# A two-layer decoder on one core: products of the identity with itself where the plan of work gives TensorE nothing

## What is computed

```python
x = _layernorm(x + _L0_attn_ref(x, ...))            # attention by random features
x = _layernorm(x + _L0_xattn_ref(x, ctx_768, ...))  # attention over the text, then an MLP
x = _layernorm(x + _L0_ffn_ref(x, ...))             # router, 8 experts with capacity, top 2
x = _layernorm(x + _L1_attn_ref(x, ...))            # causal attention by a Taylor expansion
x = _layernorm(x + _L1_xattn_ref(x, ctx_768, ...))  # attention over the text, 16 heads of 64
x = _layernorm(x + _L1_ffn_ref(x, ...))             # causal attention, then 4 dense experts
```

## Time and profile before

| | us |
|---|---|
| median of 3 runs | 1166.63 |
| the 3 runs | 1166.63, 1165.93, 1173.93 |
| span of the profiled execution | 1165.0 |
| PE busy | 1001.8 (86%) |
| DVE busy | 640.4 (55%) |
| ACT busy | 588.3 (50%) |
| POOL busy | 284.6 (24%) |
| share of the chain that ended last: PE, DVE, ACT | 56%, 19%, 11% |

### The profile page before, as it was taken

One profiled execution on the slowest core, in us unless ns is written; L12 is line 12 of the kernel. 1 busy time (PEld: TensorE's weight loads), 2 busy tenths in 40 slices (PEclk: granted clock), 3 DMA queues, 4 the chain that ended last, 5 costly groups with the idle time before them and its releaser, 6 DMA issues.

```text
span 1165.0 us, 21556 instructions
## 1 busy us (share of the span) xinstructions
PE 1001.8 (86%) x8624; PEld 707.4 (61%) x8624; DVE 640.4 (55%) x1519; ACT 588.3 (50%) x1374; POOL 284.6 (24%) x292
## 2 busy tenths in 40 slices
PE   7996898887689988789998799889888897789995
PEld 4664565665388854456655676667666665447654
DVE  3246545666669833454455476776676664527003
ACT  5532565552468844344544354556555544465741
POOL 2521412100500033211112202221132124132733
PEclk9988889898989999899999988999999888679998
DMA  9341464102679785422252243313222105000001
GB/s 311 99 86 40 112 127 110 45 12 98 209 272 314 259 278 168 139 88 85 80 173 88 81 120 105 101 34 107 81 57 78 27 1 226 1 1 1 1 1 32
DMA packets 66676, 123.68 MB, mean 106 GB/s; under 512 B 11632, under 2 KB 41968, under 8 KB 62496
## 3 DMA queue, kind: packets, MB, share of 16 engines
q1 hardware_dynamic: 64528, 117.48, 33.0%
q0 software_dynamic: 2048, 4.82, 1.4%
HBM read 86.30 MB, written 35.92 MB: 105 GB/s over the span
## 4 chain that ended last, share of the span: by engine, by line
PE 56%; DVE 19%; ACT 11%; DMA 5%; issue 4%; POOL 4%; SPq 1%; another core or an unknown queue 0%; DVEq 0%; ACTq 0%; POOLq 0%
PE psum L398 38%; DVE s_p L2695 3%; ACT s_p L2653 3%; POOL rs L2985 2%; PE psum L2612 2%; DVE s_max L2684 2%; PE psum L2623 2%; PE psum L1369 2%; PE psum L2784 1%; DVE s_pT L2676 1%; PE psum L550 1%; DVE s_max L653 1%; PE psum L2173 1%; PE psum L2159 1%; PE psum L2604 1%
## 5 line engine op out<-in xcount | busy, mean ns | idle before, releaser
L2653 ACT ACTIVATE s_p<-psum,s_max 112x375 f32<-112x375 f32 x128 | 72.3, 569 | 87.6 <-DVE s_max L2684 87.6
L693 POOL TENSOR_TENSOR rstd<-meanvar,minus_half 112x1 f32<-112x1 f32 x40 | 23.1, 578 | 279.6 <-DVE meanvar L645 209.9
L653 DVE TENSOR_REDUCE s_max<-psum 112x2 f32<-112x750 f32 x64 | 59.4, 935 | 32.5 <-PE psum L550 31.4
L2985 POOL TENSOR_TENSOR rs<-ms,minus_half 112x32 f32<-112x32 f32 x8 | 43.5, 5442 | 110.3 <-DVE ms L2919 110.3
L398 PE MATMUL psum<-Wv,ctx 128*125 128x512 f16 x240 | 59.6, 392 | 11.2 <-ACT s_v L624 5.4
L398 PE MATMUL psum<-ctx,Wk 128*128 128x375 f16 x320 | 62.8, 331 | 5.0 <-ACT s_yT L2242 2.8
L2684 DVE TENSOR_REDUCE s_max<-psum 112x1 f32<-112x375 f32 x128 | 63.7, 539 | 2.3 <-PE psum L2604 2.1
L2612 PE MATMUL psum<-ident,s_p 112*125 112x112 f32 x384 | 61.4, 294 | 3.9 <-DVE s_p L2695 2.3
L609 ACT ACTIVATE s_k<-psum 128x375 f16<-128x375 f32 x64 | 31.2, 488 | 62.1 <-PE psum L398 59.5
L2604 PE MATMUL psum<-s_k,s_q 64*112 64x375 f16 x384 | 46.0, 345 | 17.0 <-ACT s_p L2653 6.5
L2612 PEld LDWEIGHTS psum<-ident,s_p 112*125 112x125 f32 x384 | 51.7, 198 | 13.7 <-DVE s_p L2695 3.9
(11 more groups left out here) (360 smaller groups left out, 2445.1 us busy)
## 6 DMA issues: line engine op xcount, KB each, us to landing
keys<-s_k SPq DMA_DIRECT2D x64, 187.5 KB, 2.2
s_k<-keys SPq DMA_DIRECT2D x8, 1500.0 KB, 7.6
values<-s_v SPq DMA_DIRECT2D x48, 224.0 KB
s_v<-values SPq DMA_DIRECT2D x16, 672.0 KB
raw_wg<-in_wg SPq DMA_DIRECT2D x8, 1024.0 KB, 6.6
raw_wu<-in_wu SPq DMA_DIRECT2D x8, 1024.0 KB, 7.1
raw_wd<-in_wd SPq DMA_DIRECT2D x8, 1024.0 KB
s_kd<-k_halves SPq DMA_DIRECT2D x48, 93.8 KB, 3.8
```

Source lines behind the costliest of these rows:

```text
L653: VE.tensor_reduce(s1_max[b % 2][:, 2 * p:2 * p + 2], rings["s1"][unit][0:N, :, 0:S], X, ALU.max, negate=True).then_inc(*V.up("max1", n))
L2653: SC.activation(rings["p4"][2 * n + j], rings["s4"][(n, j)][0:N, 0:S], ACT.Exp, bias=s4_max[b % 2][:, h:h + 1], accum_out=s4_sum[b % 2][:, ...
L2985: GP.tensor_tensor(rs5[b % 2][:], ms5[b % 2][:], minus_half[:], ALU.pow).then_inc(*G.up("rs5", b))
```

## The change

`weave` gets a parameter `idle` with the name of a ring. Whenever all strands have passed once, and some bank of that ring is free by the plan, it places a unit `("warm", i)` that takes a bank of that ring. In TensorE's program such a unit waits for the last reader of the bank and issues five products of the identity (128x128, f32) with 64 of its own columns into the bank. Nothing reads them; the unit has no mark, and the bank counts as free again at once. The three `weave` calls of stages 1, 3 and 4 pass `misc1`, `misc3` and `misc4`. Nothing else moves: apart from the inserted products PE's order is the same, and so is that of DVE, ACT, POOL and SyncE. The plan places 61 such units, 305 matmuls of the program: 19 in stage 1, 12 in stage 3, 30 in stage 4.

```diff
+    WARM = 5
+    warm_units = (("warm", i) for i in itertools.count())
+    step("warm", bank="warm")
+
-    def weave(*streams, filler=iter(())):
+    def weave(*streams, filler=iter(()), idle=None):
...
                 hurry[0] = passed >= len(live)
+                if idle and passed == len(live) and any(
+                        all(name in r.value for r, name in freed) for freed in rings[idle].freed):
+                    rings["warm"] = rings[idle]
+                    place(next(warm_units))
                 units = next(stream, "end")
...
+    def keep_busy(unit, ring):
+
+        pe.wait_ge(*ring.free(unit))
+        for _ in range(WARM):
+            TE.matmul(ring[unit][:, 0:64], ident[:], ident[:, 0:64], start=True, stop=True)
...
-          follow(s1_queries, range(2, B, 2)))
+          follow(s1_queries, range(2, B, 2)), idle="misc1")
...
-            if what == "v1":
+            if what == "warm":
+                keep_busy(unit, rings["misc1"])
+            elif what == "v1":
...
-          filler=keys4)
+          filler=keys4, idle="misc3")
...
-          s5_split())
+          s5_split(), idle="misc4")
```

More of the change, by code:

```diff
@@ L2136, in tensor_s3 @@
             what, *at = unit
-            if what == "qk3":
+            if what == "warm":
+                keep_busy(unit, rings["misc3"])
+            elif what == "qk3":
                 b, c = at
@@ L2594, in tensor_s4 @@
             what, *at = unit
-            if what == "sc4":
+            if what == "warm":
+                keep_busy(unit, rings["misc4"])
+            elif what == "sc4":
                 n, = at
```

## The result

Slower: 1211.9 us, median of four runs (1194.8 to 1225.0), against 1166.7 for the kernel before, run beside it (four runs, 1165.9 to 1173.9). The ratio is 1.0263, 95% interval 1.0184 to 1.0342: clear of no change, but it does not decide whether the loss is over 2%. Times 1166.7 the ratio is 1197 us. The profiled execution of the changed kernel took 1214.1 us with a span of 1212.2.

What follows compares the result with a forecast made beforehand. PE, busy 86% of the span with 56% of the last chain, was taken as the bound; 1165.0 + 10.5 + 6.6 + 2.0 = 1184.1 us profiled, with 1.6 for the median of runs 1185.7, range 1169 to 1206.

Steps and rivals of the forecast that it cites:

- The price of a unit: Everywhere: ten traced products with their weight loads take 1.1 us at 2.4 GHz, 2.1 at 1.2 GHz.
- The reading of the eight router products: End of stage 1: eight router products take 0.95 us; weight loads, 0.11 us each, set the pace, not the columns.
- the first rival: All three ends: products stream at the columns' pace, a unit costs 0.6 us, 1164 us in all; chance 0.15.
- End of stage 1, +10.5: 11 units before the last router product add 8.9 us, four units ahead of them 1.6; sum +10.5 us.
- The rival that stage 2 absorbs the delay: Stage 2 waits for expert weights or values rather than the router, so 1175 us; chance 0.07.
- End of stage 3, +6.6: Five units before the `w_Wo` products add 4.0 us, three later ones 2.6; the clock is high, nothing to win back.
- End of stage 4, +2.: Units add 2.6 us at `w_wo` and 2.2 behind it; stage 6 gives back 2.0 and 0.8; sum +2.0 us.
- if the units hold the clock at 2.4 GHz: End of stage 4, ahead of `w_wo`: with the clock held, busy time at 1.2 GHz shrinks, winning 12.0 us.
- the rival that they do not: End of stage 4: thin products don't hold the clock, 1220 us, or 1203 for half of it; chance 0.15 together.
- The reading of the clock: From the profile rows: the clock falls after waits of 1 to 3 us and is high where products are dense.
- Behind it, -2.0 and -0.8: Stage 6: first 12 products drop from 4.44 to about 2.2 us (-2.0); the 36 from 1031.79 give -0.8.
- The bank waits: Stages 1 and 3: units make PE wait for unneeded bank readers, tenths each, 1190 us; counted within the forecast's 0.60.

Runs made afterwards that it cites:

- narrow kernel: Changed kernel with 64 stationary identity columns instead of 128, units at all three ends: 1166.8 us in one run; timed again, median 1179.9, ratio 0.9982 to before.
- narrow units in stage 4 alone: Units of five f32 products with 64 stationary columns instead of 128, only at the end of stage 4: ratio 0.9954 to before, median 1167.5 us.

## Why the forecast was right, and where it was too low

Direction and most of the mechanism came out as forecast: units fill the waits, what does not fit into them delays the path, and each end stands for itself. What did not is that the units would hold the clock at the end of stage 4. The forecast was 1185.7 us, +19.1 on the profiled execution. By ratio the changed kernel took 1197, inside the range of 1169 to 1206; the plain median of its four runs, 1211.9, lies above it. The working, step by step:

- **The price of a unit**, 1.1 us at 2.4 GHz and 2.1 at 1.2: measured 1.10 and 2.05 to 2.09. The reading of the eight router products held, and with it the first rival fell: no unit of the changed kernel is near 0.6. The narrow kernel shows why. The isolated gap of the Trainium skill, "TensorE: Matmul & The Clock Gate", section "Back-to-back issue gap", would have made a unit as cheap as that bound or cheaper; the same section says that this gap counts too little for small products, since it leaves out the weight loads, and the 0.11 us per product measured here agrees with that.
- **End of stage 1, +10.5:** +9.7. The last router product ends 9 us later than the start of the stretch alone would put it, the `out` product that ran at the low clock took 1.93 where it had 3.48, the value products behind the five last units took 3.40 where they had 5.72, and those five units cost next to nothing, as forecast. The granted clock over this end is 1.00, where before some 10 of its 36.7 us ran at 1.2 GHz; even with that gain it is longer. The rival that stage 2 absorbs the delay fell with the run that has units in stage 1 alone.
- **End of stage 3, +6.6:** +7.4. There was no low clock to win back, as forecast.
- **End of stage 4, +2.** This is the term that was mis-sized: +11.8 up to the first product of stage 6 where the steps had +4.8 (2.6 and 2.2), and +1 to +4 behind it where they had -2.8. The parts can be read from the stretches. The units: forecast 30 x 1.1 = 33; in the trace 26 at 1.10 and four at 2.07, 37.0. The idle time filled: forecast 14.8 + 2.2 less 0.8 of latency, 16.2; measured 18.8 - 4.0 = 14.8. The clock: forecast 12.0 back; PE's work other than units went from 37.1 to 63.7 - 37.0 = 26.7, so 10.4 came back. 37.0 - 14.8 - 10.4 = 11.8. The difference of 7.0 is 4.0 + 1.4 + 1.6, and the first and the last of these have one cause: 17.1 us of the stretch ran at 1.2 GHz in one piece, four units among them. The step that failed is "if the units hold the clock at 2.4 GHz"; I named the rival that they do not, and gave it 0.15, but let no part of its price into the sum. The step was true by half: 37 us low before, 18 after.
- **The reading of the clock.** The prediction says that the clock falls after waits of 1 to 3 us. The rows are not that simple: at the end of stage 3 waits up to 2.45 us left it at 1.00, while in the changed kernel it fell at 1032.4, and the only wait of the 10 us ahead of it is one of 0.68 us. The second pair of rows is the same place in the kernel with narrow units in stage 4 alone, where PE idled longer and the clock stayed up:

```profile
1031.52 1.04 PE L2804 MATMUL psum<-k,q 32*112 32x224 f32 x8 [0.68 <-ACT e_up L2851]
1032.49 0.99 PE L2807 MATMUL psum<-mask,ident 112*112 112x448 bf16 x2
```

```profile
999.66 1.01 PE L2804 MATMUL psum<-k,q 32*112 32x224 f32 x8 [1.21 <-ACT e_up L2851]
1000.60 0.58 PE L2807 MATMUL psum<-mask,ident 112*112 112x448 bf16 x2
```

- **Behind it, -2.0 and -0.8:** the first twelve products took 4.64 us, still at 1.2 GHz, in a low stretch of 17 us of their own; nothing came back. No kernel of the table has stage 6 below 136.8 us, so at most 0.3 of these 2.8 us came back anywhere. In the kernel with units in stage 4 alone the low stretches there are shorter (10 us) and stage 6 costs +1.1. How this falls out is not decided by the units at hand, and it stays open.
- **The bank waits:** the ends are explained without them. The kernel with one product in a unit has the same waits, and its first two ends are only 2.2 and 1.1 us longer, no more than its products take; so they cost next to nothing.
- **The base.** Of the 47.2 us between the two profiled executions, 32.6 lie in the ends and stage 6, and 14.6 in columns of the table where no instruction was added. Against the second trace of before the same sum is 33.3 and 2.4. That part goes with where the clock was low: its mean over the first of these columns was 0.90 before and 0.87 in the changed kernel, over the third 0.98 and 0.95, and the second trace of before has 0.95 there as well, without any unit. A forecast from one profile inherits it. An estimate from the table: 1173.5, the usual time of before, and the 32.6 us of the ends give 1206.

What stays open is why the clock stays low for 17 us at the end of stage 4 with five-product units while PE is busy all of the time, and does not with the narrow ones, which occupy PE for less, nor with ten. The runs show that it does, repeatably (twice at the same place, three times not at all with the narrow units), not what separates them.

## What to carry to other kernels

A filler that keeps TensorE awake is paid per unit wherever the wait is shorter than the unit, and it can earn only where the clock was low: check both before placing it. Here two of three ends had waits of 0.6 to 2.7 us mostly at 2.4 GHz, and every filler tried there made them longer; at the third, with units there alone, wide bf16 units of 0.22 and 0.43 us and narrow f32 ones of 0.63 beat the kernel before (0.9937 to 0.9954), and f32 units of 1.1 us lost 0.9%. A wide bf16 product here kept PE at work over 512 columns for 0.22 us, with one weight load, a thin f32 one over 64 columns for the same time, with two; the intervals do not tell the wide fillers from the narrow ones. Time a filler over many runs: the first four of before lay 7 us below the medians of the later ones.

## What the runs showed that was not expected

- A full PE does not mean a high clock: with PE busy 17.10 of 17.10 us, half of it with the filler, the granted clock stayed at 0.50 in two kernels. Before, showed the milder case, 14.10 of 17.07.
- Halving the stationary columns of a thin f32 product took a unit of ten from 1.10 to 0.63 us, while a product over 512 moving columns in bf16 cost 0.22: eight times the columns at the price of two loads of 128 f32 columns.
- One kernel on one core, unchanged, spread from 1160.2 to 1186.2 us over 27 executions, with mean clocks that differ (0.916 to 0.939). In its two traces the clock falls at other places, and the 288 to 636 us stretch is 13.9 us longer in one than in the other; the three ends repeated to 0.6 us all the same.
